# Two gated attention and feed-forward layers: tokens in two halves, attention units between the gate and up products

## What is computed

```python
x = x + tanh(g_xattn[0]) * L0_xattn(layernorm(x), ctx, ctx)   # 32 query heads of 8, 8 key heads
x = x + tanh(g_ffn[0])   * L0_ffn(layernorm(x))   # down(silu(gate(x)) * up(x)), 256 -> 704 -> 256, int weights
x = x + tanh(g_xattn[1]) * (L1_xattn(layernorm(x), ctx, ctx) @ Wc.T + bc)   # 16 heads of 16, 4 groups
x = x + tanh(g_ffn[1])   * L1_moe(layernorm(x))   # 32 experts, 256 -> 96 -> 256, the 8 best by softmax weight
```

## Time and profile before

| | |
|---|---|
| median of 3 runs | 449.8 us (447.51 to 450.45) |
| the profiled execution | 450.2 us from first to last instruction |
| TensorE busy | 399.1 us, 89% |
| VectorE busy | 296.7 us, 66% |
| ScalarE, GpSimd busy | 198.7 and 180.4 us |
| weights loaded | 30 loads of 384 KB, 3.1 us each to landing |

### The profile page before, as it was taken

How to read it: one execution, slowest core, us unless ns; L and a number is a source line. 1 busy time by engine, 2 the same in 40 slices (tenths; PEclk the granted TensorE clock), 3 DMA queues, 4 the chain that set the end, 5 groups by cost and what they waited for, 6 DMA issues and landing times.

```text
span 450.2 us, 6432 instructions
## 1 busy us (share of the span) xinstructions
PE 399.1 (89%) x2032; PEld 327.9 (73%) x2032; DVE 296.7 (66%) x554; ACT 198.7 (44%) x382; POOL 180.4 (40%) x174
## 2 busy tenths in 40 slices
PE   0598888959999778898877999999999999999994
PEld 0497777848888478787664887887887887887883
DVE  5989899843555778996465366566566566566554
ACT  6465455735444635554136333433433433333332
POOL 8776667561788353447500231131131121221200
PEclk9999899998999989999688899999999999999999
DMA  6500000110202000001100112112112011111002
GB/s 169 133 1 2 1 0 1 35 37 1 71 0 95 0 0 2 1 1 35 37 0 0 36 35 71 35 35 73 35 36 69 35 40 65 35 43 62 0 1 93
DMA packets 10711, 15.99 MB, mean 36 GB/s; under 512 B 4097, under 2 KB 6657, under 8 KB 10689
## 3 DMA queue, kind: packets, MB, share of 16 engines
q1 hardware_dynamic: 10688, 15.71, 11.8%
HBM read 14.66 MB, written 1.05 MB: 35 GB/s over the span
## 4 chain that ended last, share of the span: by engine, by line
PE 72%; DVE 15%; issue 5%; POOL 4%; ACT 2%; DVEq 1%; DMA 1%; POOLq 0%; ACTq 0%
PE bank L1002 19%; PE bank L1003 18%; PE bank L1004 18%; PE bank L1080 5%; PE bank L1055 4%; PE bank L1064 3%; DVE mx L734 2%; DVE dt_pt L739 2%; DVE xn L722 1%; POOL rstd L405 1%; DVE yt L762 1%; PE bank L1027 1%; DVE x L976 1%; PE bank L1040 1%; PE bank L1096 1%
## 5 line engine op out<-in xcount | busy, mean ns | idle before, releaser
L427 POOL TENSOR_TENSOR wl<-wraw,wh 128x768 fp32r<-128x768 f32 x24 | 44.7, 1863 | 162.2 <-ACT wh L551 162.2
L1002 PE MATMUL bank<-xh,wh 128*128 128x512 f32 x240 | 96.3, 401 | 0.0
L1003 PE MATMUL bank<-xl,wh 128*128 128x512 f32 x240 | 95.6, 398 | 0.0
L1004 PE MATMUL bank<-xh,wl 128*128 128x512 f32 x240 | 95.5, 398 | 0.0
L655 ACT ACTIVATE hh<-h_t 128x512 fp32r<-128x512 f32 x60 | 37.9, 632 | 114.9 <-DVE h_t L888 101.3
L893 DVE TENSOR_TENSOR hl<-h_t,hh 128x512 fp32r<-128x512 f32 x60 | 48.6, 810 | 42.7 <-ACT hh L655 42.7
L883 DVE TENSOR_TENSOR t_t<-bank,pts 128x512 f32<-128x512 f32 x48 | 33.2, 692 | 43.5 <-PE bank L1004 42.1
L888 DVE TENSOR_TENSOR h_t<-t_t,vbd 128x512 f32<-128x512 f32 x48 | 53.4, 1113 | 3.1 <-DVE t_t L883 1.0
L1055 PE MATMUL bank<-kbd,qt 128*128 128x256 f32 (+2 forms) x128 | 36.8, 395 | 20.2 <-DVE dt_pt L739 17.3
L1002 PEld LDWEIGHTS bank<-xh,wh 128*128 128x128 f32 x240 | 46.5, 194 | 9.9 <-issue 0.2
L1004 PEld LDWEIGHTS bank<-xh,wl 128*128 128x128 f32 x240 | 46.3, 193 | 10.1
(11 more groups left out here) (104 smaller groups left out, 577.9 us busy)
## 6 DMA issues: line engine op xcount, KB each, us to landing
wraw<-w SPq DMA_DIRECT2D x30, 384.0 KB, 3.1
out<-x SPq DMA_DIRECT2D x8, 128.0 KB, 1.8
x<-x_in SPq DMA_DIRECT2D x1, 768.0 KB, 6.8
ctx_k<-ctx_t SPq DMA_DIRECT2D x2, 256.0 KB, 3.8
ctx_v<-ctx_in SPq DMA_DIRECT2D x2, 256.0 KB, 8.3
x<-x_in SPq DMA_DIRECT2D x1, 256.0 KB, 2.7
wc<-wc_t SPq DMA_DIRECT2D x1, 256.0 KB, 2.9
vbd<-sel_in SPq DMA_DIRECT2D x1, 256.0 KB, 3.5
```

The costliest lines, as they stand in the source:

```text
L427: nc.gpsimd.tensor_tensor(wl[:, cc % WRING, :], src[:, cc % 2, :], wh[:, cc % WRING, :].bitcast(F32), ALU.subtract).then_inc(m.w_split, 1)
L1002: nc.tensor.matmul(o, wh[:, s, w_sl], rh, start=first, stop=False, skip_group_check=reopened)
L1003: nc.tensor.matmul(o, wh[:, s, w_sl], rl, start=False, stop=False, skip_group_check=reopened)
L1004: return nc.tensor.matmul(o, wl[:, s, w_sl], rh, start=False, stop=last, skip_group_check=reopened)
```

## The change

The tokens are cut into two halves of four tiles. There are four feed-forward passes: layer 0 for half 0 (steps 0 to 5), layer 0 for half 1 (6 to 11), the mixture for half 0 (12 to 35), the mixture for half 1 (36 to 59). A step is one chunk for one half, the same 18 matmuls as one block before. Attention is cut into ticks: a tick n of an engine is its work around unit n, the engines at different lags, and VectorE, ScalarE and GpSimd run one tick ahead of TensorE in the passes. Ticks 0 to 21 of attention 0 run alone on TensorE (0 to 22 on the others); the rest stand in steps 0 to 5, those of attention 1 for half 0 in steps 9 to 11 and a tail after step 11, those for half 1 in steps 16 to 32. In a step all of them stand between gate and up product. Steps 36 to 59 hold none.

PSUM: gate and up now have one bank each; attention has one bank for scores, one for transposes, one for values, and a second one of each only up to unit 20 of layer 0. Values have 72 columns instead of 128. Key blocks are made in a ring of three tiles. Layer 0's weights stay in six slots for both passes; the mixture's 24 chunks are streamed twice, 54 loads in all, into three raw buffers, three steps ahead. The split of transposed x goes from GpSimd to ScalarE (high part) and VectorE (`x_low`). The first layer norm's statistics are taken for one tile a tile (`ln_stats` in tick u = 1). Silu is made from tanh: ScalarE computes tanh of half the gate, VectorE multiplies (tanh + 1) by the gate from PSUM (`gate`), and then by up. The mask stays in one PSUM bank, spread every third step, and `weigh` reads it there. `scales`, some short operations on constants and the copy of the selection matrix, moves into tick 12. The first half's output is stored before the load with index 42. The routing is made twice, for half the tokens each (after step 11 and before step 34).

The tables, the banks of units, and which unit's scores must be used up before a unit's scores may start (`before`):

```diff
+VW = 72
...
+PASS = ((0, F0), (F0, 2 * F0), (2 * F0, 2 * F0 + MC), (2 * F0 + MC, 2 * F0 + 2 * MC))
...
+GB, UB, MASK = 0, 1, 7
+DB = ((2, 3), (2, 3), (2, 3), (4, 5))
+SB, PB, VB, MB = 4, 5, 6, 7
...
+TWO = 20
+X_TWO = 4
+
+
+ALONE = 22
+BESIDE0 = {0: ((22, 23, 24), ()), 1: ((25, 26, 27), ()), 2: ((28, 29, 30), ()), 3: ((31, 32, 33), ()),
+           4: ((34, 35), ()), 5: ((36, 37), ())}
+BESIDE1 = {9: ((0, 1), ()), 10: ((2, 3, 4, 5), ()), 11: ((6, 7, 8, 9, 10), ())}
+BESIDE2 = {s: ((s - 16,), ()) for s in range(16, 33)}
+BESIDE = (BESIDE0, BESIDE1, BESIDE2)
+START = {9: 0, 15: 1}
+TAIL = ((11, 12), (13, 14, 15, 16))
+ROUTE = (13, 34)
...
+    def before(self, n):
+
+        return n - 2 if self.layer == 0 and n <= TWO else n - 1
+
+    def s_bank(self, n):
+        return GB if self.doubled(n) and n % 2 else SB
```

SyncE's loads and stores, and ScalarE's gate:

```diff
+            def load(i):
+                if i >= WRAW:
+                    sp.wait_ge(F.wf_ready if i - WRAW < F0 else F.w_split, i - WRAW + 1)
+                dst, src = (wrawi, w0[i:i + 1]) if i < F0 else (wraw, w1[(i - F0) % MC:(i - F0) % MC + 1])
+                sp.dma_start(dst[:, i % WRAW, :], src.rearrange("a p n -> (a p) n")).then_inc(F.w_loaded[i % WRAW], 16)
...
+            for i in range(2, LOADS):
+                if i == LOADS - MC + 12:
+                    store(0, HT)
+                load(i)
+            store(HT, TT)
```

```diff
+            def gate(s):
...
+                nc.scalar.activation(s_t[:, s % 2, :], bank[GB][:], ACT.Tanh,
+                                     scale=sgh[:, c:c + 1] if s < MOE0 else 0.5).then_inc(F.s_ready, 1)
```

VectorE, the two ticks and the loop over the steps:

```diff
+            def maximum(a, n):
+                dve.wait_ge(a.scored, n + 1)
+                s = bank[a.s_bank(n)][:].rearrange("p (h t) -> p h t", t=KEYS)
+                return chains[a.layer].mark(ops.reduce_max(mx[:, n % 2, :], s, AX.X))
+
+            def shift(a, n, done):
+                chains[a.layer].wait(done)
+                if n >= 2:
+                    dve.wait_ge(a.p_ready, n - 1)
+                ops.tensor_tensor(dt_[:, n % 2, :].rearrange("p (h t) -> p h t", t=KEYS),
+                                  bank[a.s_bank(n)][:].rearrange("p (h t) -> p h t", t=KEYS),
+                                  mx[:, n % 2, :].unsqueeze(2).to_broadcast([P, 8, KEYS]), ALU.subtract
+                                  ).then_inc(a.sub_done, 1)
...
+            def x_low(a, t):
+                dve.wait_ge(a.xh_ready, t + 1)
+                tok = slice(t * P, (t + 1) * P)
+                ops.tensor_tensor(xl[:, :, tok], bank[a.x_bank(t)][:, 0:DM].rearrange("p (k c) -> p k c", c=P),
+                                  xh[:, :, tok].bitcast(F32), ALU.subtract).then_inc(a.xl_ready, 1)
...
+            def tick0(n):
+                a, (t, u) = A[0], divmod(n, 4)
+                if n < a.total:
+                    done = maximum(a, n)
+                if u == 0 and 0 <= t - 1 < TT:
+                    normalise(a, t - 1, 0)
+                if u == 0 and 0 <= t - 2 < TT:
+                    next_apply(a, t - 2)
+                if u == 1 and t + 2 < TT:
+                    if t == 0:
+                        dve.wait_ge(x_loaded[1], 16)
+                    ln_stats(a, t + 2, t + 3)
+                if u == 2 and 0 <= t - 1 < TT:
+                    normalise(a, t - 1, 1)
+                if u == 2 and 0 <= t - 2 < TT:
+                    x_low(a, t - 2)
+                if u == 3 and 0 <= t - 1 < TT:
+                    next_stats(a, t - 1)
+                if u == 3 and t + 2 < TT:
+                    layer_norm(a, t + 2)
+                if n < a.total:
+                    shift(a, n, done)
+                if n == 12:
+                    scales()
...
+            def tick1(h, i):
+                a, (t, u), t0, n = A[1], divmod(i, 2), h * HT, h * HT * 2 + i
+                if i < 2 * HT:
+                    done = maximum(a, n)
+                if u == 1 and 0 <= t - 3 < HT:
+                    residual(t0 + t - 3)
+                if 0 <= i - 3 < 2 * HT:
+                    normalise(a, (n - 3) // 2, (n - 3) % 2)
+                if u == 1 and 0 <= t - 3 < HT:
+                    next_stats(a, t0 + t - 3)
+                if u == 0 and 0 <= t - 4 < HT:
+                    next_apply(a, t0 + t - 4)
+                if u == 0 and 0 <= t - 5 < HT:
+                    x_low(a, t0 + t - 5)
+                if i < 2 * HT:
+                    shift(a, n, done)
+                if u == 0 and t + 2 < HT:
+                    layer_norm(a, t0 + t + 2)
...
+            def gate(s):
+                k = s % 2
+                dve.wait_ge(F.s_ready, s + 1)
+                ops.scalar_tensor_tensor(t_t[:, k, :], s_t[:, k, :], 1.0, bank[GB][:], ALU.add, ALU.mult
+                                         ).then_inc(F.sg_done, 1)
...
+            def weigh(s):
+                k = s % 2
+                dve.wait_ge(F.m_done, s + 1)
+                dve.wait_ge(R.spread_done, (pass_of(s) - 2) * QUADS + quad(s) + 1)
+                ops.tensor_tensor(h_t[:, k, :], bank[MASK][:], t_t[:, k, :], ALU.mult).then_inc(F.h_full, 1)
...
+            for s in range(STEPS):
+                if s and not (last(s - 1) and s == PASS[2][0]) and s != ROUTE[0]:
+                    split_h(s - 1)
+                if s == 8:
...
+                if s in START:
+                    tick1(START[s], 0)
+                for k, n in beside(s, 0):
+                    tick(k, n + 1)
+                gate(s)
+                multiply(s)
```

TensorE:

```diff
+            def scores(a, n):
+                t = a.tile(n)
...
+                if a.before(n) >= 0:
+                    pe.wait_ge(a.sub_done, a.before(n) + 1)
...
+            def tick0(n):
+                a, (t, u) = A[0], divmod(n, 4)
+                if u == 2 and t + 1 < TT:
+                    q_transposes(a, t + 1)
+                if u == 1 and 0 <= t - 2 < TT:
+                    x_transposes(a, t - 2)
+                if n + 1 < a.total:
+                    scores(a, n + 1)
+                if 0 <= n - 2 < a.total:
+                    values(a, n - 2)
+                if n < a.total:
+                    p_transposes(a, n)
...
+            def gate(s):
...
+                if s == 0:
+                    pe.wait_ge(A[0].sub_done, TWO)
+                else:
+                    pe.wait_ge(F.sg_done, s)
...
+            for n in range(ALONE):
+                tick0(n)
+            for s in range(STEPS):
+                gate(s)
+                if s in START:
+                    scores(A[1], START[s] * 2 * HT)
+                for k, n in beside(s, 0):
+                    tick(k, n)
+                up(s)
...
+                if s and s != MOE0:
+                    down(s - 1)
...
+                if s == MOE0 - 1:
+                    down(s)
+                    for n in TAIL[0]:
+                        tick1(0, n)
+                    back(1)
+                    for n in TAIL[1]:
+                        tick1(0, n)
+            down(STEPS - 1)
+            back(3)
```

More of the change, by code:

```diff
@@ L45, with beside, pass_of, last @@
 HIDDEN = 704
-FFN_CHUNKS = (HIDDEN + P - 1) // P
+F0 = (HIDDEN + P - 1) // P
+MC = EXPERTS * INNER // P
 NEG = -3.0e38
[L48 to L91, removed]
+VW = 72
+RING = 3
+SLOTS = 6
+WRAW = 3
+PASS = ((0, F0), (F0, 2 * F0), (2 * F0, 2 * F0 + MC), (2 * F0 + MC, 2 * F0 + 2 * MC))
+MOE0 = 2 * F0
+STEPS = 2 * F0 + 2 * MC
+LOADS = F0 + 2 * MC
+GB, UB, MASK = 0, 1, 7
+DB = ((2, 3), (2, 3), (2, 3), (4, 5))
+SB, PB, VB, MB = 4, 5, 6, 7
+BACK = ((5, 6), (5, 6), (2, 3), (2, 3))
+TWO = 20
[9 more added lines that the diff above has]
+ROUTE = (13, 34)
+PREP = 3
+def beside(s, place):
+    return [(k, n) for k, table in enumerate(BESIDE) if s in table for n in table[s][place]]
+def pass_of(s):
+    return next(p for p, (a, b) in enumerate(PASS) if a <= s < b)
+def last(s):
+    return s + 1 == PASS[pass_of(s)][1]
+def quad(s):
+    return (s - PASS[pass_of(s)][0]) // CPQ
 class Chain:
     def __init__(self, eng, sem):
-        self.eng, self.sem, self.base, self.n = eng, sem, 0, 0
-    def at(self, base):
-        self.base, self.n = base, 0
+        self.eng, self.sem, self.n = eng, sem, 0
     def mark(self, ins):
@@ L998, in _ @@
+            split_h(STEPS - 1)
+            take_out(3)
+            add_back(3)
         @block.tensor
         def _(pe):
[L1000 to L1004 removed]
@@ new lines, in values @@
+            def values(a, n):
+                b2, gps = a.part(n)
+                t = a.tile(n)
+                q = 2 * t + b2
+                if n == 0:
+                    pe.wait_ge(a.v_ready, a.hk)
+                    pe.wait_ge(a.ones_ready, a.hk)
+                if gps[0] == 0 and a.v_before(q) >= 0:
+                    pe.wait_ge(a.y_done, a.v_before(q) + 1)
+                for j in range(4):
+                    gp, pair = gps[j // a.npair], j % a.npair
+                    if j in (0, 2):
+                        pe.wait_ge(a.pts_ready, 2 * n + 1 + j // 2)
```

(3 more changed lines are left out.)

1555 lines of the change are left out of this document (746 added, 809 removed).

## The result

The changed kernel takes 475.2 us (median of 4 runs, 471.4 to 475.9); the kernel before took 448.7 beside it. The ratio is 1.056, 95% interval 1.050 to 1.061: slower. The forecast was 463, slower. Executions over 1.5% above the fastest of their kernel are left out of the ratios, and since run 8's trace shows one of them, no stretch of it is read.

What follows compares the result with a forecast made beforehand. TensorE was taken to bound the feed-forward stages and VectorE attention; in the weave, VectorE's loop on one score bank. Stretches from start through passes, tail, routing and end were summed to 463 us, own range 453 to 475.

Steps and rivals of the forecast that it cites:

- Gate product 0: Start and attention 0's ticks 0 to 22 alone: first gate product may start at 80.6 us, VectorE's additions lengthening each tile.
- Pass 0: Steps 0 to 5 with ticks 23 to 38 woven in, paced by VectorE's one-bank loop: 54.5 us, to 135.1.
- Steps 6 to 8: Steps without ticks, pass 0's output turned back and normalised between products: 15.5 us, to 150.6.
- Steps 9 to 11 and the tail: Attention 1 for half the tokens, one-bank loop, then drain ticks and a serial end: 56.4 us, to 207.
- Routing and steps 12 to 15: First routing 13.7 us plus 2.4 for the half clock, then steps to the end of 15: 25.5 us in all.
- Steps 16 to 32: One attention tick a step, VectorE's loop 6.3 to 6.8 against TensorE's 6.1 to 6.5: 104 us, to 336.5.
- Steps 33 to 35: Three steps of 4.1 and 3 for the second routing: 15.5 us, to 352.
- Pass 3: Last 24 steps at 4.1, with 2 for masks and 2.3 for turning pass 2's output: 101 us, to 453.
- TensorE the bound: Rival: VectorE's woven loop is shorter than TensorE's part, so the weave fills TensorE's gaps: 434 us, chance 0.14.
- Additions in VectorE's idle tenth: Rival: added VectorE work falls into its idle time, tiles stay near 10.2: 450 us, no change, chance 0.17.
- Lower clock through the weave: Rival: TensorE stays at 1.2 GHz in woven ticks and steps, becoming the bound: 485 us, chance 0.11.
- Late weights: Rival: streamed weights arrive late, 0.5 us a step over 48 steps: 487 us, chance 0.03.

Runs made afterwards that it cites:

- run 8: Changed kernel with all ticks of attention 0 before the first gate product (no weave), units 20 to 31 on one score bank: 481.9 us, ratio 1.068.
- run 5: Changed kernel with VectorE's order in one-bank ticks made maximum, shift, then the rest (normalising, statistics, x's operations): 464.2 us, ratio 1.027.
- run 12: run 8 (no weave, one score bank) with VectorE's order of run 5, maximum, shift, rest: 468.5 us, ratio 1.040.
- run 4: Changed kernel with all ticks of attention 0 before the first gate product (no weave) and two score banks to the end: 474.1 us, ratio 1.046.
- run 1: Changed kernel with the up and down products of steps 0 to 5 and 9 to 11 dealt out between ticks: 474.6 us, ratio 1.053.
- sixth run: run 5 plus products dealt out as in run 1, first scores ahead of the gate product, low part after the first tick's shift: 457.8 us, 1.015.
- run 2: Changed kernel with ScalarE building the values of attention 1 in step 6 instead of tick 20: 476.5 us, ratio 1.061.
- run 7: Changed kernel plus 39 matmuls on unused data after ticks of step 11 and the tail, to keep the clock up: 473.1 us, ratio 1.051.
- run 3: Changed kernel with the mask-spreading matmul contracted over 128 rows, the upper 64 zero, instead of 64: 474.8 us, ratio 1.051.
- run 10: run 9 plus attention 1's values built in step 6 and masks over 128 rows, zeros written by ScalarE in step 7: 457.7 us, ratio 1.013.
- run 9: sixth run with the output of pass 1 turned back in step 12 instead of between the tail's ticks: 458.1 us, ratio 1.016.
- run 11: run 10 plus 18 matmuls on unused data, three after each tick of the tail: 457.5 us, ratio 1.013.

## Why the prediction came out as it did

The sign and the mechanism were right, and shown for the woven ticks: they run in a ring of one score bank on VectorE's queue (waits in the profile after; runs 5 and 12 shorten the ring by order alone; runs 4 and 8 show that the bank in the old order takes back what the weave hides; run 1 that dealing out TensorE's products changes nothing). What is lost ahead of unit 20, where the forecast has VectorE's additions, is read off the shifts only: no run took them out. Nor was it found what the sixth run still lacks, 7 us to the kernel before. Term by term, on the profiled execution, forecast and measured:

- Gate product 0 at 80.6: **83.8**. Unit 19 is shifted at 71.1, as forecast; the tile of units 8 to 12 costs 1.0 more (forecast 1.25). Ticks 20 to 22 were forecast at 3.4, 3.0 and 3.1 and took 3.8, 3.4 and 5.3: in tick 20 normalising and `xm` (1.13 us) stand between maximum and shift, TensorE is idle for 2.42 and then runs at a clock of 0.55 to 0.76, which I had not counted. I put this on ScalarE's values of attention 1 in the second run; but the wait ends before they begin and is there without them (run 2), and with them in place and the other order the clock stays at 1.00 (run 5). With that order the three ticks take 1.9, 2.7 and 2.2 (run 5); the half clock's part wasn't tried by itself.
- Pass 0, 54.5: **54.8**. Steps 6 to 8, 15.5: **14.7**.
- Steps 9 to 11 and the tail, 56.4: **66.2**. This is the term that was mis-sized. Up to the shift of tick 7 it is 32.5 against 32.6 (eight ticks and two step changes); behind it 33.7 against 23.6. I had charged the half clock to the routing's first down product alone (2.4), reading as a matter of that place, though the tail before it leaves TensorE as idle. Of the 10.1, 6.7 stand in the drain ticks and the last products (185.81 to 204.96, where I had 12.5), at a granted clock of 0.74 from 185 to 205 us; run 7, at 1.00 there, is 3.3 shorter in this stretch, and what makes up the rest of it is open. The other parts are the chain itself: my sum left out the additions of pass 1's output with their transposes (209.98 to 211.97 on the chain, 2.0) and took ticks 12 and 13 at 3.5, which last 5.0 here and in run 7 alike.
- Routing and steps 12 to 15, 25.5: **25.4**.
- Steps 16 to 32, 104: **99.9**. TensorE is full here, 10.0 of 10 us in most windows, and paces the eight steps with ticks at 6.3; I had put VectorE's 6.6 above it. My 104 is also mis-added: its parts make 52.8 + 8.5 + 42.4 + 2.4 = 106.1, and the whole sum 465 instead of 463. The split's meetings with GpSimd's subtraction lengthened VectorE's operations by 6.4 over all 60 steps, nearly all of it here, where I had 2.4. Steps 33 to 35, 15.5: **14.0**.
- Pass 3, 101: **103.5**. Steps of 4.08, 4.08 and 4.73: the mask's matmul, which I priced at a quarter of a microsecond, costs 0.64 (run 3).
- End, 10.4: **10.4**.

Sum of the differences: 3.2 + 0.3 - 0.8 + 9.8 - 0.1 - 4.1 - 1.5 + 2.5 = 9.3, of the 9.6 between 463 and 472.6. That the total is no further off owes something to luck: the two largest terms miss in opposite directions, +9.8 and -4.1.

The rivals. *TensorE the bound* (434): its condition was a tick under 2.0; shifts inside a woven step stand 2.3 to 3.8 us apart and 4.4 to 8.0 where a step changes, and run 1 changed nothing. *Additions in VectorE's idle tenth* (450): a tile is 1.0 longer. *Lower clock through the weave* (485): not in the weave (1.00 from 100 to 125 us), but in the ticks just before it and in the tail, where I had not put it; its price, as worded, adds 12 and not 6 for the products, which makes 491. *Late weights* (487): steps of 4.08, and GpSimd waits for ScalarE's copies (87.7 us in all), not the reverse. The values' 72 columns, taken at 0, are worth 0.05 a unit:

```profile
175.38 0.84 PE bank L1054 x8
```

That is 0.84 for eight, against 0.89 with 128. The Trainium skill (TensorE: Matmul & The Clock Gate, "LDWEIGHTS (loading the stationary operand)") gives 107 ns a load, 0.86 for eight by an estimate from it; the trace agrees.

## What to carry to other kernels

Two engines with gaps in the same stretch can be a ring and not spare room: before weaving more work into it, follow one turn of it in the timeline, and put every instruction that is not on the ring behind the one that frees the shared buffer. Here that order, with no instruction added or taken away, was worth 11 us, and in the run without a weave made one bank as good as two. And price a serial tail at the clock that TensorE will have there: here it was 0.69, and the sum had the full one.

## What the runs showed of the hardware

**Two engines' meeting.** The low part takes 0.69 alone. When GpSimd's subtraction of weights runs, up to the whole of that is added. First the changed kernel in step 19, then step 34 of run 10, which lasts 2.0 longer there:

```profile
263.18 1.85 POOL L436 TENSOR_TENSOR wl<-wraw,wh 128x768 fp32r<-128x768 f32 x1
263.57 2.01 DVE L873 TENSOR_TENSOR hl<-h_t,hh 128x512 fp32r<-128x512 f32 x1 [0.70 <-ACT hh L532]
```

```profile
339.09 1.93 POOL L437 TENSOR_TENSOR wl<-wraw,wh 128x768 fp32r<-128x768 f32 x1 [2.51 <-ACT wh L533]
339.27 2.29 DVE L893 TENSOR_TENSOR hl<-h_t,hh 128x512 fp32r<-128x512 f32 x1
```

VectorE's operation began after GpSimd's and ends 0.55 and 0.54 after it. This bears out the rule of the Trainium skill (SBUF — State Buffer, "Who interferes with whom"). In step 34 of the changed kernel VectorE began first, at 352.23, 0.20 ahead of GpSimd: its operation took 0.68 and GpSimd's 2.19. So 0.4 us in the order of two starts made 1.6 of the 2.0 there. The 27 us more that the prediction worked out for a meeting in every step stayed away because few splits fall into a subtraction: of the 17 in steps 16 to 32, four took 1.94 to 2.01 and three 0.94 to 1.06.

**A matmul over half the rows** costs 0.64 in a stream of products at 0.23, 0.41 more than one over all rows with zeros in the upper half (run 3). The Trainium skill (TensorEngine Tiling (Array Packing), "Key Properties") states that a change of tiling mode drains TensorE; that this matmul is such a change is my reading, the price is the trace's.

**The clock** follows the order of another engine: around units 20 to 22 the changed kernel's TensorE was granted 0.74, after it had waited 2.42 us for a shift, and in run 5, where VectorE's order alone is another and the waits are 0.22 and 0.47, 1.00 (windows in run 5). From 70 to 84 us the traces with the old order on one bank have 0.72 to 0.76 (runs 1, 3 and 7; run 2, without the values, 0.88), those with the new order 0.98 to 1.00 (runs 6 and 9 to 12).
